# State space scan with routed experts on one core: VectorE's work in a chunk of the scan in a new order, the state step fused, x stored turned, rows loaded in one DMA

## The reference

```python
xn = layernorm(x)
x = xn @ Wx.T; z = xn @ Wz.T                      # 512 wide
x = silu(causal_conv(x, conv_w, conv_b))
b = x @ Wb.T; c = x @ Wc.T; dt = softplus(x @ Wdt.T + b_dt)   # 8 heads, 64 states
state = exp(dt_t * a) * state + (dt_t * b_t) x_t  # scan over 4096 steps
y_t = c_t . state
out = (groupnorm(y + d * x) * silu(z)) @ Wout.T
g = silu(experts(xn))                             # each expert takes its top 1024 of 8192 tokens
result = input + out * g
```

## Time and profile before

| what | us |
|---|---|
| runs, median of 3 (lowest to highest) | 1244.86 (1244.12 to 1245.27) |
| the profiled execution, its own time | 1243.34 |
| its span, from the first to the last instruction | 1241.2 |
| PE busy | 1208.3 (97%) |
| PEld busy | 1009.3 |
| DVE busy | 966.1 (78%) |
| ACT busy | 614.1 |
| POOL busy | 798.1 |

### The profile page before, as it was taken

The page is one execution under the profiler, slowest core; times in us unless marked ns, Lnnn a source line. Parts: engine busy times, 40 slices in busy tenths (PEclk is TensorE's granted clock), DMA queues, the critical chain, the costliest instruction groups (busy, mean ns, idle before and its releaser), DMA issues.

```text
span 1241.2 us, 30788 instructions
## 1 busy us (share of the span) xinstructions
PE 1208.3 (97%) x12207; PEld 1009.3 (81%) x12207; DVE 966.1 (78%) x1909; ACT 614.1 (49%) x1276; POOL 798.1 (64%) x788
## 2 busy tenths in 40 slices
PE   8999999999999999999999998899999999999998
PEld 4666677888878888878878886789999889899998
DVE  7999878899787777776777777897778766776676
ACT  6999974434444444434444444434344332554453
POOL 4889845555555568667766656476666654576764
PEclk9999999999999999999999999999999999999999
DMA  9799757755445554465544545464444545799995
GB/s 295 263 339 361 292 187 178 194 157 162 140 145 166 161 154 131 151 178 157 153 129 138 180 154 175 156 156 85 105 101 91 103 86 117 231 323 329 337 322 172
DMA packets 183662, 231.34 MB, mean 186 GB/s; under 512 B 53984, under 2 KB 153568, under 8 KB 177248
## 3 DMA queue, kind: packets, MB, share of 16 engines
q1 hardware_dynamic: 170368, 212.09, 53.2%
q0 software_dynamic: 12288, 17.05, 8.0%
q10 hardware_dynamic: 864, 0.24, 0.1%
HBM read 147.81 MB, written 81.53 MB: 185 GB/s over the span
## 4 chain that ended last, share of the span: by engine, by line
PE 79%; DVE 10%; ACT 3%; issue 3%; DMA 2%; POOL 1%; SPq 1%; POOLq 0%; ACTq 0%; DVEq 0%
PE ps L1362 24%; PE ps L1708 9%; PE ps L1965 9%; PE ps L2199 7%; PE ps L2178 7%; PE ps L1443 4%; PE ps L1410 3%; PE ps L1432 3%; PE ps L1470 2%; PE ps L1454 2%; PE ps L1481 2%; PE ps L680 2%; DVE state L1085 2%; DVE acc L312 1%; ACT tap L489 1%
## 5 line engine op out<-in xcount | busy, mean ns | idle before, releaser
L1329 ACT ACTIVATE decay<-tap,ncum 128x128 f32<-128x128 f32 x344 | 105.5, 389 | 134.5 <-POOL tap L1240 134.5
L1893 POOL DMA_INDIRECT ffn_dram<-ob,idx x64 | 110.3, 1723 | 81.6 <-DVE ob L1812 67.8
L1927 ACT ACTIVATE mid<-ps,b_up 128x512 f32<-128x512 f32 x96 | 66.0, 689 | 156.7 <-PE ps L1708 135.3
L1247 POOL TENSOR_TENSOR x_lo<-x,x_hi 128x512 fp32r<-128x512 f32 x56 | 75.9, 1356 | 94.3 <-ACT x_hi L1313 94.2
L1269 POOL TENSOR_SCALAR yb<-x,dcol 128x512 f32<-128x512 f32 x64 | 44.8, 701 | 85.9 <-DVE ystat L1135 58.3
L1362 PE MATMUL ps<-x_hi,w_hi_b 128*128 128x512 f32 x240 | 99.3, 414 | 0.6 <-ACT bT L1318 0.6
L1362 PE MATMUL ps<-x_hi,w_hi_c 128*128 128x512 f32 x240 | 99.2, 413 | 0.0
L2054 POOL TENSOR_SCALAR yc<-yc,gn_scale,gn_shift 128x512 f32<-128x512 f32 x56 | 76.2, 1373 | 33.8 <-DMA yc<-y_dram 33.8
L1362 PE MATMUL ps<-x_lo,w_hi_b 128*128 128x512 f32 x240 | 94.6, 394 | 2.1 <-issue 2.1
L1362 PE MATMUL ps<-x_lo,w_hi_c 128*128 128x512 f32 x240 | 94.1, 392 | 0.0
L1257 POOL TENSOR_TENSOR c_dec<-cT,ecum_row 128x512 f32<-128x512 f32 x64 | 82.3, 1286 | 17.9 <-PE ps L1454 16.0
(11 more groups left out here) (319 smaller groups left out, 4026.7 us busy)
## 6 DMA issues: line engine op xcount, KB each, us to landing
tap<-cum_dram SPq DMA_DIRECT2D x86, 256.0 KB, 4.1
x_dram<-x SPq DMA_DIRECT2D x16, 1024.0 KB, 5.5
ecum_row<-ecum_dram SPq DMA_DIRECT2D x128, 128.0 KB
y_dram<-yb SPq DMA_DIRECT2D x16, 1024.0 KB, 4.7
yc<-y_dram SPq DMA_DIRECT2D x16, 1024.0 KB, 6.6
cum_row<-cum_dram SPq DMA_DIRECT2D x42, 256.0 KB
rows_dram<-xn SPq DMA_DIRECT2D x16, 512.0 KB, 3.2
x<-x_dram SPq DMA_DIRECT2D x16, 512.0 KB, 4.2
```

What stands on the lines that cost most here:

```text
L1247: nc.gpsimd.tensor_tensor(low, raw, high, ALU.subtract).then_inc(x_lo_ready, 1)
L1329: n = nc.scalar.activation(decay[g % 2][:, h, :], cum_row[g % NR][:, row, :], ACT.Exp, bias=t.ncum[:, g, h:h + 1])
L1893: pool.indirect_dma_start(out=t.ffn_dram, out_offset=bass.IndirectOffsetOnAxis(ap=t.idx[:, e, h * HC + c:h * HC + c + 1], axis=0), in_=ob[ ...
```

## The change

On DVE, a chunk g of the scan now begins with `x_dt` and `mix` of chunk g; only then comes the end of chunk g-1, in the new function `finish`: the state, the lists, and both halves of y. The state step is fused: the scaling of all 256 columns and the addition give way to four instructions of 64 columns, each (state times decay) plus product. After `finish` come `b_w`, the threshold round, `list_slots` and `bn_stats`. The rounds move one chunk later, into chunks 1 to 15, on PE too, and their preparation (`begin`) moves from ahead of chunk 0 into it. The last chunk's end is called after the loop.

In the front, `silu` writes x2 turned, so that `x2_dram` holds x turned, PE's product for dt (L709) reads the odd quarters with swapped halves and writes them back in order, all later loads of x2 are one DMA with long runs instead of five, and the one load of block 0 in the front (`x0_raw`) becomes the one with five DMAs. `cum` is kept with the heads in the order in which the scan's rows are wanted, so `load_cum` is one DMA instead of two; for this DVE copies `cum` in two halves and ACT makes `ecum` in two halves. POOL's and PE's waits on these loads count accordingly.

```diff
@@ -72,6 +72,18 @@
 TURNED = 16 * 5
+def tile_parity(ap):
+    return ap.rearrange("p t (a k i) -> p k t a i", a=2, k=2)
+def by_tile_pair(ap):
+    return ap.rearrange("p t (k a i) -> p k t a i", a=2, k=2)
@@ -424,12 +434,15 @@
             psc = [ps_t[i][:, 0:NT * H].rearrange("p (t h) -> p t h", h=H) for i in range(2)]
-            do(v.tensor_copy(t.cum[:, :, :], psc[0]), "cum")
+            cum = by_tile_pair(t.cum[:, :, :])
+            for k in range(2):
+                do(v.tensor_copy(cum[:, k], tile_parity(psc[0])[:, k]), "cum")
             dve.wait_ge(ten, 2)
-            do_turned(lambda o, a, b: v.tensor_tensor(o, a, b, ALU.subtract), gap, psc[1], t.cum[:, :, :], name="gap")
+            do_turned(lambda o, a, b: v.tensor_tensor(o, a, b, ALU.subtract), tile_parity(gap), tile_parity(psc[1]), cum,
+                      name="gap")
             do(v.tensor_copy(gates_g[:, :, :, :], t.gates[:, :, :].rearrange("p (q g) e -> p g q e", g=GT)),
                "gates_g")
-            do_turned(lambda o, a: v.tensor_scalar(o, a, -1.0, None, ALU.mult), t.ncum[:, :, :], t.cum[:, :, :],
+            do_turned(lambda o, a: v.tensor_scalar(o, a, -1.0, None, ALU.mult), tile_parity(t.ncum[:, :, :]), cum,
                       name="ncum")
@@ -494,7 +508,7 @@
                     act.wait_ge(thin_ready, b)
-                nc.scalar.activation(x2[b % 2][:, m, :], acc[:, m, :], ACT.Silu).then_inc(x2_ready, 1)
+                nc.scalar.activation(*t.turned(x2[b % 2][:, m, :], acc[:, m, :], m % 2), ACT.Silu).then_inc(x2_ready, 1)
@@ -571,11 +585,12 @@
                 tile_copy(n)
-            act.wait_ge(x2_back[1], TURNED)
+            act.wait_ge(x2_back[1], 16)
             for m in range(MT):
...
             act.wait_ge(vec, steps["cum"])
-            nc.scalar.activation(ecum, t.cum[:, :, :], ACT.Exp).then_inc(sca, 1)
+            nc.scalar.activation(tile_parity(ecum)[:, 0], by_tile_pair(t.cum[:, :, :])[:, 0], ACT.Exp)
+            nc.scalar.activation(tile_parity(ecum)[:, 1], by_tile_pair(t.cum[:, :, :])[:, 1], ACT.Exp).then_inc(sca, 1)
             act.wait_ge(vec, steps["gap"])
@@ -706,7 +721,8 @@
                     pe.wait_ge(x2_ready, MT * (b - 1) + m + 1)
-                    mm = pe.matmul(bank[m * LANE:(m + 1) * LANE, :], wdt[:, m, cols], x2[(b - 1) % 2][:, m, :],
+                    out, x = t.turned(bank[m * LANE:(m + 1) * LANE, :], x2[(b - 1) % 2][:, m, :], m % 2)
+                    mm = pe.matmul(out, wdt[:, m, cols], x,
                                    start=(b == NB), stop=(b % 2 == 1 or b == NB), skip_group_check=True)
@@ -840,11 +856,11 @@
                     sp.wait_ge(x2_stored[0], 16)
-                    sp.dma_start(x0_raw, t.x2_dram[0]).then_inc(x0_loaded, 16)
+                    t.load_turned(sp, x0_raw, t.x2_dram[0], x0_loaded)
                 if b >= NB - 2:
...
                     sp.wait_ge(thin_ready, b + 2)
-                    t.load_turned(sp, x2[b % 2], t.x2_dram[b % 2], x2_back[b % 2])
+                    sp.dma_start(x2[b % 2][:, :, :], t.x2_dram[b % 2]).then_inc(x2_back[b % 2], 16)
             for p in range(2):
@@ -1082,12 +1098,11 @@
                 dve.wait_ge(state_ready, updates(g))
-                v.tensor_tensor(state[:, :, :], state[:, :, :],
-                                t.dec[:, g:g + 1, :].rearrange("p a m -> p m a").to_broadcast([P, MT, HD]),
-                                ALU.mult).then_inc(state_scaled, 1)
-                dve.wait_ge(state_scaled, updates(g) - g // SPAN)
                 dve.wait_ge(s_mm, updates(g) + 1)
-                v.tensor_tensor(state[:, :, :], new, state[:, :, :], ALU.add).then_inc(state_ready, 1)
+                for m in range(MT):
+                    n = v.scalar_tensor_tensor(state[:, m, :], state[:, m, :], t.dec[:, g, m:m + 1], new[:, m, :],
+                                               ALU.mult, ALU.add)
+                n.then_inc(state_ready, 1)
@@ -1103,15 +1118,41 @@
+        def finish(g):
+            b, c = g // CH, g % CH
+            cols = slice(c * P, (c + 1) * P)
+            dve.wait_ge(y_mm, g + 1)
+            update(g)
+            if LIST0 <= g < LIST1:
+                add_lists(g - LIST0, g)
+            if c == 0:
+                dve.wait_ge(dx_ready, b + 1)
+            y_out, (y_0, y_1) = yb[b % 2][:, :, cols], [a[:, :].rearrange("p (m n) -> p m n", m=MT) for a in ps_y]
+            v.tensor_tensor(y_out, y_0, y_out, ALU.add).then_inc(y_step, 1)
+            dve.wait_ge(y_step, g + 1 + g // SPAN + 1)
+            v.tensor_tensor(y_out, y_1, y_out, ALU.add).then_inc(y_ready, 1)
+        def begin():
+            do(v.memset(thr[:, :], 0))
+            high, low = (t.cst[:, C_BIT + i:C_BIT + BITS:2] for i in range(2))
+            do(v.tensor_copy(tries[:, :, 0], low))
+            do(v.tensor_copy(tries[:, :, 1], high))
+            do(v.tensor_tensor(tries[:, :, 2], low, high, ALU.add))
+            count(0)
         def chunk(g):
             b, c = g // CH, g % CH
-            cols = slice(c * P, (c + 1) * P)
             last = g % SPAN == SPAN - 1
             dve.wait_ge(x_turned, g + 1)
+            until(dve, y_mm, g)
             x_heads = ps_xb[:, :].rearrange("p (h n) -> p h n", h=H)
...
             if g % SPAN == 0:
+                if g:
+                    finish(g - 1)
                 clear_y(g)
@@ -1119,16 +1160,20 @@
                                 decay[g % 2][:, 4 * i:4 * i + 4, :], ALU.mult).then_inc(mix_ready, 1)
-            if LIST0 - 1 <= g < LIST1 - 1:
-                list_slots(g - LIST0 + 1)
+            if g % SPAN:
+                finish(g - 1)
             if not last:
...
                                 ALU.mult).then_inc(b_w_ready, 1)
-            if g < ROUNDS:
-                next_bits(g)
+            if g == 0:
+                begin()
+            elif g <= ROUNDS:
+                next_bits(g - 1)
+            if LIST0 - 1 <= g < LIST1 - 1:
+                list_slots(g - LIST0 + 1)
             if b:
@@ -1142,35 +1187,18 @@
                     x.middle(dve, 0, f)
-            dve.wait_ge(y_mm, g + 1)
-            if c == 0:
-                dve.wait_ge(dx_ready, b + 1)
-            if LIST0 <= g < LIST1:
-                add_lists(g - LIST0, g)
-            y_out, (y_0, y_1) = yb[b % 2][:, :, cols], [a[:, :].rearrange("p (m n) -> p m n", m=MT) for a in ps_y]
-            v.tensor_tensor(y_out, y_0, y_out, ALU.add).then_inc(y_step, 1)
-            update(g)
-            dve.wait_ge(y_step, g + 1 + g // SPAN + 1)
-            v.tensor_tensor(y_out, y_1, y_out, ALU.add).then_inc(y_ready, 1)
...
         dve.wait_ge(t.front_sca, 8)
-        do(v.memset(thr[:, :], 0))
-        high, low = (t.cst[:, C_BIT + i:C_BIT + BITS:2] for i in range(2))
-        do(v.tensor_copy(tries[:, :, 0], low))
-        do(v.tensor_copy(tries[:, :, 1], high))
-        do(v.tensor_tensor(tries[:, :, 2], low, high, ALU.add))
-        count(0)
         for g in range(NT):
             chunk(g)
+        finish(NT - 1)
...
             until(sp, exp_ready, g - NR + 1)
-            by_tile = t.cum_dram[g].rearrange("(a k i) c -> k a (i c)", a=2, k=2)
-            for k in range(2):
-                sp.dma_start(cum_row[g % NR][:, k * H // 2:(k + 1) * H // 2, :], by_tile[k].partition_broadcast(P)
-                             ).then_inc(cum_loaded[g % NR], 16)
+            sp.dma_start(cum_row[g % NR][:, :, :], t.cum_dram[g].partition_broadcast(P)).then_inc(
+                cum_loaded[g % NR], 16)
@@ -1417,8 +1445,8 @@
             pe.wait_ge(b_w_ready, updates(g) + 1)
-            if g < ROUNDS:
-                pe.wait_ge(bit_step, 4 * g + 2)
+            if 1 <= g <= ROUNDS:
+                pe.wait_ge(bit_step, 4 * (g - 1) + 2)
             elif SLOTS < g < SLOTS + CH:
@@ -1481,8 +1509,8 @@
             until(pe, state_ready, updates(g))
-            if g < ROUNDS:
-                total(g)
+            if 1 <= g <= ROUNDS:
+                total(g - 1)
             elif SLOTS <= g < SLOTS + CH:
```

More of the change, by code:

```diff
@@ L390, in do, with do_turned @@
                     steps[name] = done[0]
-            def do_turned(op, *aps, name):
-                parts = [a.rearrange("p t (a k i) -> p k t a i", a=2, k=2) for a in aps]
+            def do_turned(op, *parts, name):
                 do(op(*(a[:, 0] for a in parts)))
@@ L443, in _ @@
             do(v.tensor_copy(t.gateT[:, :], ps_x[3][:, 0:SEG]), "gateT")
-            do_turned(lambda o, a: v.tensor_copy(o, a), t.dt[:, :, :], w1, name="dt")
+            do_turned(lambda o, a: v.tensor_copy(o, a), tile_parity(t.dt[:, :, :]), tile_parity(w1),
+                      name="dt")
         @block.scalar
@@ L537, in _ @@
                     m = X0_AT.index(b)
-                    act.wait_ge(x0_loaded, 16)
+                    act.wait_ge(x0_loaded, TURNED)
                     nc.scalar.activation(t.x_hi[0][:, m, :], x0_raw[:, m, :], ACT.Copy).then_inc(x0_hi, 1)
@@ L927, in phase_scan @@
```

(16 more changed lines are left out.)

## The result

The changed kernel takes **1238.61 us**, the median of six runs (1235.46 to 1240.59), against 1245.07 for the kernel before (six runs, 1242.96 to 1247.15). The ratio is 0.9945, 95% interval 0.9928 to 0.9962: 6.5 us less. The prediction was 1239.1, faster. The profiled execution took 1240.59 us with a span of 1238.4; it is the slowest of the six, and why it is will matter.

What follows compares the result with a forecast made beforehand. PE, busy 97% of the span, was taken as the bound, so only its idle time could be won. -6.9 + 0 + 2.2 - 1.1 = -5.8 us against the 1244.86 median gave 1239.1 us, range 1236 to 1242.

Steps and rivals of the forecast that it cites:

- Part 1: From 200 to 740 us, PE's eight waits for DVE's x_dt go: -6.9 us.
- rival E: The waits stay, as some other DVE instruction takes over the long hold-up: about 1244 us, no change; chance 0.03.
- The state's margin: In some 58 chunks, state ready for PE at 3.47 us, needed at 3.58: 0.11 us to spare.
- rival A: DVE's fused instructions don't overlap, state too late by 0.21 to 0.27 us in 58 chunks: about 1253 us; chance 0.11.
- C: Rival: POOL holds DVE's fused step through its scalar column: some +25 us, 1264 us; chance 0.04.
- rival B: Slower hand-over to PE or later mix eats the state's margin: 0.05 us a chunk, +2.9, about 1242 us; chance 0.14.
- Part 2: The 1.4 us wait behind the copies of the lists stays, losing as much as now: 0.
- Part 3: The last chunks, 60 to 63, get slower, with b_w behind the state and both halves of y: +2.2 us.
- Part 4: Start of the scan: x2 there sooner and ncum shorter, so PE's gap in chunk 0 goes: -1.1 us, bounds 0 and -2.5.
- Part 5: The front: same instructions with swapped reads, block 0 in five DMAs, PE's swapped read for dt: 0, bounds to +9.
- Rival D: PE's swapped read in the product for dt is slow: +3 to +9 us, 1245 us; chance 0.05.

## Why the prediction was right, and where it was not

**Part 1 (the eight waits, -6.9): right.** Measured -7.1. The mechanism is shown from both sides: with the fused step alone the waits go, and with the new order but not the fused step the kernel takes 22.7 us more than with both. No second long hold-up took their place, so rival E is out. What I hadn't seen is that the order did nothing for it. The prediction's own rows would have told: in the chunk of the earlier trace rows x_dt ended 4.19 us in, and PE could have gone on at 3.40. The scaling and the addition took 2.13 + 0.42 there, and four fused instructions take 0.92 by the prediction's estimate, 1.6 less, which puts x_dt at 2.6. In the run with the fused step alone it is ready at 2.45 in chunk 27, and PE goes on to B's transposes at 3.25, without a wait.

**The state's margin: right, and larger.** 0.85 us instead of 0.92, ready at 3.34 instead of 3.42: a fused instruction takes 0.274 instead of 0.29, and they are (0.85 - 0.274) / 3 = 0.19 us apart. The margin is 0.19, not 0.11; six pieces instead of four used it up. Rivals A (no overlap) and C (held by POOL through its scalar column) are out: of 480 fused instructions in two kernels none took over 279 ns, in the old place beside c_dec too. These runs agree with the rule of the Trainium skill that the prediction weighed (SBUF — State Buffer, Who interferes with whom): the scaling, with two inputs in SBUF, is stretched beside POOL, and the fused step isn't. From the Trainium skill's section The DRAIN you can't avoid (VectorE: DVE Perf Modes) the prediction took only that a next instruction waits for an empty pipeline, and made that its case for rival A. The same paragraph goes on that a next instruction that is not held starts earlier, and that is what these runs show: 0.19 us apart at 0.274 long. Of rival B's mechanism the run with six pieces gives the price: 0.05 to 0.06 us a chunk for a state 0.26 later.

**Part 2 (the chunk behind the copies, 0): right.** 10.80 us against 10.82; x_dt starts at 2.60 and the state is ready at 5.25, as forecast. The working as written doesn't add up: copies from 5.9 that take 5.51 end at 11.4, not 11.7. In the trace they start at 6.09, behind a small operation of 0.27 us that the sum left out, and end at 11.66.

**Part 3 (the last chunks, +2.2): right in its waits, wrong in its sum.** The update of chunk 60 starts at 5.41 (predicted 5.4). With the clock held up chunk 60 lasts 7.96 us, 0.59 more than before, against +0.6 predicted; the waits of chunk 61 grow by (1.39 + 2.09) - (0.71 + 0.37 + 1.67) = 0.73, those of 62 and the rest add 0.5 and 0.2: +2.0 in all. (With two operations, in a profile whose clock stayed up there, chunk 61 lasts 9.77 us, 0.63 more than before.) But the profile has +6.1. The missing term is the clock. Faster x_dt moved PE's transposes of B ahead, to 1.44, so that the two idle stretches of 1.20 and 1.23 us in chunk 60 became one of 3.32, and from there on the matmuls ran at half clock in this execution. With the stretch filled, 2.13 us of the excess are gone. I had added idle time and never asked in how many pieces it comes. The times go with the clock: among the six, those with a mean clock of 1.000 took 1235.46 and 1236.14 us, the one with 0.999 1238.04, and those with 0.994 to 0.997 1239.18 to 1240.59. So the term belongs to a part of the executions; where the clock fell in the three others below 1.000 isn't known.

**Part 4 (the start of the scan, -1.1): right.** Chunks 0 and 1 together are 1.2 shorter, 1.15 of it in chunk 0 by the loads alone. This is shown in the length of the chunks only; the whole time with the loads alone doesn't show it. The three ncum instructions take 2.17 us instead of 4.11, and mix waits 1.94 instead of 2.74.

**Part 5 (the front, 0): right within what can be seen.** PE's swapped read costs nothing: L725 is busy for 17.7 us with 594 ns each, as L709 was the earlier trace rows. Rival D is out.

**Why the total fits so well** is partly luck. At a mean clock of 1.000 the change is worth about 8 us (1235.5 and 1236.1 against 1242.9, 1243.1, 1244.9 and 1245.6, the runs of before with that clock beside the later experiments, and 1243.3, its profiled execution), more than the 5.8 of the sum. Some 2 us of this are PE's waits for nothing visible, three in the profile before (chunks 17, 35 and 46) and one after. The lower clock of the other four runs takes 2 to 5 us back. Neither term is in the sum, though the prediction's range allowed for the first.

## What to carry to other kernels

When an engine is late because one instruction is sometimes stretched, take away what stretches it before changing the order: the fused step alone gave as much as the whole change, and the order and the loads without it lost 15 us. A schedule that is good where PE is full can be bad where it has gaps: cost the ends of the loop separately, and put the first thing that the other engine lacks first there. Count idle time of TensorE by the length of each stretch, not only by its sum, since the matmuls behind a long one may run at half clock; and before one part of a chain is made shorter or spread out, ask who waits for its last piece.

## What the runs showed of the hardware

**The clock fell behind idle stretches, in most cases and not always.** Each of the three profiles with one of 3.3 to 3.6 us in chunk 60 (the changed kernel, the order with two operations, six pieces) shows it there, but two of the changed kernel's six runs have a mean clock of 1.000. Of the twenty of 1.9 to 2.7 us in the scans of the thirteen profiles, thirteen have it (1.90 at 343 us and 2.09 in chunk 61 of the changed kernel, 2.73 in the run with the tail put back) and seven don't: with the loads alone PE idled 2.31 us in chunk 61 and the clock stayed at 1.00. The kernel before had its mean clock between 0.996 and 1.000 from run to run, and its times follow it: 1244.8 to 1249.6 at 0.996 and 0.997, 1242.4 to 1246.6 at 0.999 and 1.000. What decides between the cases wasn't found.

**PE's waits for nothing visible have a companion.** In the eight that I looked at, in six kernels (1.3 to 3.0 us long), one packet of instructions, 0.02 MB, landed as a burst of other transfers ended, at most 2 us ahead of the gap or early in it. In all thirteen profiles, 23 waits of this kind last over 0.8 us between 200 and 735 us, and each has such a packet that began at most 1.5 us before it or in its first 0.7 us. But such packets are common, 68 in each of the two main profiles from 190 to 820 us, and most stand beside no wait. The packet ahead of the changed kernel's wait at 343.14 us, in the DMA view from 342 to 343 us:

```profile
q1 hardware_dynamic: 74, 0.24, 59.5%
q8 instruction: 1, 0.02, 5.9%
```

That these waits are instructions that arrive late behind the loads fits, and explains why they move between chunks (35 and 46 in the old order, 16 and 17 in the new), but it is only argued: no run here moved a load away from one.
